# A macaron block of two expert layers and a scan layer: steps spread over other slots, the down projection turned round

## The reference, cut to what matters

```
x = x + 0.5 * ffn(layernorm(x))      # f = 0
x = x + mamba(layernorm(x))
x = x + 0.5 * ffn(layernorm(x))      # f = 1, same weights

ffn:   router = x @ Wg; top 2 of 8 experts, softmax of their logits -> w (tokens x 8)
       y  = sum_e w_e * (silu(x @ W1_e) * (x @ W2_e)) @ W3_e      (H = 176)
       y += (silu(x @ Ws1) * (x @ Ws2)) @ Ws3                      (HS = 352)
mamba: x_in, z = split(x @ W_in + b_in);  xc = silu(conv4(x_in) + conv_b)
       B, C = split(xc @ W_xp + b_xp);  delta = softplus(xc @ W_dt + b_dt)
       h_t = exp(delta_t * A) * h_{t-1} + delta_t * xc_t * B_t     (16 states)
       y_t = sum_s h_t[s] * C_t[s];  y = (y + D * xc) * silu(z)
       out = layernorm_ab(x + y @ W_out + b_out)
```

## Time and profile before

| what | us |
|---|---|
| median of three runs | 2236.86 |
| lowest and highest of them | 2232.0 and 2238.75 |
| the profiled execution | 2241.29 |
| its span, first to last instruction | 2239.5 |
| first scan of the first group starts at | 148.2 |
| twelve full iterations, k = 2 to 13 | 358.6 to 1942.5 |
| mean granted clock of TensorE, of full speed | 0.887 |

### The profile page before, as it was taken

One profiled execution on the slowest core, in us unless ns is written; L12 is line 12 of the kernel. 1 busy time (PEld: TensorE's weight loads), 2 busy tenths in 40 slices (PEclk: granted clock), 3 DMA queues, 4 the chain that ended last, 5 costly groups with the idle time before them and its releaser, 6 DMA issues.

```text
span 2239.5 us, 22836 instructions
## 1 busy us (share of the span) xinstructions
PE 1794.9 (80%) x4674; PEld 804.4 (36%) x4674; DVE 1639.6 (73%) x2505; ACT 1535.3 (69%) x2083; POOL 1441.3 (64%) x1286
## 2 busy tenths in 40 slices
PE   3878587979888888887888798788888878885577
PEld 1433233434334333333433343333333433332233
DVE  2257878687786878878687877878778786879742
ACT  1257587777778767786876778687677867776522
POOL 3346676666667675776767666676766676676753
PEclk9989788989898898998989898898989889897698
DMA  4117565555556555555555654655556555557642
GB/s 130 45 55 178 119 164 130 144 133 143 127 142 153 130 135 134 152 132 151 152 137 129 152 143 127 151 147 140 130 131 159 131 145 138 133 122 173 150 111 61
DMA packets 119129, 300.05 MB, mean 134 GB/s; under 512 B 19184, under 2 KB 40400, under 8 KB 104656
## 3 DMA queue, kind: packets, MB, share of 16 engines
q0 software_dynamic: 18432, 125.84, 28.1%
q1 hardware_dynamic: 92672, 168.88, 24.2%
q10 hardware_dynamic: 7888, 4.09, 0.7%
HBM read 167.67 MB, written 5.24 MB: 77 GB/s over the span
## 4 chain that ended last, share of the span: by engine, by line
PE 43%; ACT 21%; DVE 17%; issue 12%; POOL 3%; ACTq 1%; DMA 1%; DVEq 0%; POOLq 0%
PE ps_y L1043 9%; PE ps_h2a L1048 6%; DVE hist L868 5%; PE ps_m L1003 5%; ACT L680 5%; PE ps_h1a L1030 4%; PE ps_h1b L1030 4%; ACT L657 4%; PE ps_h2b L1048 4%; DVE den L912 3%; ACT decay L657 3%; ACT silu L680 2%; DVE yacc L950 2%; PE ps_m L1110 2%; DVE ps_db L834 2%
## 5 line engine op out<-in xcount | busy, mean ns | idle before, releaser
L569 POOL TENSOR_TENSOR prod<-hist,crow 128x1024 f32<-128x1024 f32 x224 | 556.0, 2482 | 371.8 <-DVE hist L868 368.0
L1043 PE MATMUL ps_y<-gated,down_w 128*128 128x512 f32 (+1 forms) x896 | 517.6, 664 | 101.3 <-POOL gated L521 63.2
L868 DVE TENSOR_TENSOR_SCAN hist<-decay,ps_db 128x1024 f32<-128x1024 f32 x256 | 583.2, 2278 | 13.8 <-issue 11.3
L521 POOL TENSOR_TENSOR gated<-gated,silu 128x512 f32<-128x512 f32 x352 | 476.3, 1416 | 138.1 <-DVE gated L860 108.4
L834 DVE TENSOR_TENSOR ps_db<-du,ps_db 128x1024 f32<-128x1024 f32 x256 | 313.7, 1225 | 319.1 <-PE ps_db L1012 318.8
L657 ACT ACTIVATE decay<-delta,a_neg 128x510 f32<-128x510 f32 x512 | 338.1, 711 | 2.6
L1048 PE MATMUL ps_h2a<-xnT,up_w 128*128 128x512 f32 (+1 forms) x448 | 253.2, 649 | 53.3 <-DVE gated L860 53.3
L680 ACT ACT_TABLE_LOAD x227 | 291.2, 1283 | 5.5 <-issue 0.7
L1043 PEld LDWEIGHTS ps_y<-gated,down_w 128*128 128x128 f32 (+1 forms) x896 | 180.3, 209 | 319.3 <-issue 218.0
L1030 PE MATMUL ps_h1a<-xnT,up_w 128*128 128x512 f32 (+1 forms) x448 | 248.0, 636 | 49.7 <-ACT silu L680 48.8
L657 ACT ACT_TABLE_LOAD x217 | 278.4, 1283 | 3.8
(11 more groups left out here) (137 smaller groups left out, 2242.5 us busy)
## 6 DMA issues: line engine op xcount, KB each, us to landing
yacc<-prod POOLq DMA_DIRECT2D x112, 1024.0 KB, 9.0
crow<-c_rows SPq DMA_DIRECT2D x128, 512.0 KB, 4.2
wrow<-w_rows SPq DMA_DIRECT2D x320, 128.0 KB, 3.6
wrow<-w_rows SPq DMA_DIRECT2D x64, 224.0 KB, 3.2
wrow<-w_rows SPq DMA_DIRECT2D x64, 192.0 KB, 3.6
wrow<-w_rows SPq DMA_DIRECT2D x64, 160.0 KB, 3.4
yacc<-yacc POOLq DMA_DIRECT2D x16, 512.0 KB, 6.2
wrow<-w_rows SPq DMA_DIRECT2D x64, 96.0 KB, 3.3
```

The costliest lines, as they stand in the source:

```text
L521: nc.gpsimd.tensor_tensor(gated[:, pos % NGATE, :], gated[:, pos % NGATE, :], silu[:, (pos + NCHUNK * f_parity(k, f)) % NSILU, :], ALU.mul ...
L569: nc.gpsimd.tensor_tensor(prod[:, (pair - 1 + odd) % 2, s % 2, :, :], hist[:, s % 2, :, :], c_all, ALU.mult).then_inc(prod_done, 1)
L868: nc.vector.tensor_tensor_scan(hist[:, s % 2, :, :].rearrange("p h t -> p (h t)"), decay[:, s % NA, :, :, :].rearrange("p h b t -> p (h b ...
L1043: nc.tensor.matmul(ps_y[:], down_w[0:rd, jd, :], gated[0:rd, posd % NGATE, :], start=(posd == 0), stop=(posd == NCHUNK - 1)).then_inc(down ...
```

## The change

The steps of `PLAN` stand in other slots, and some are cut in parts.

- The units start at slots 1 to 9, 11, 12 and 14 to 16 (f = 1) and 18 to 31 (f = 0). Take, join and down projection keep their lags of 1, 2 and 4 slots and run over into the next iteration.
- The down projection and the output projection are turned round: the tokens are the stationary operand, 128 at a time, and the weights move, 128 columns at a time. The result has tokens on partitions. The steps `y0`, `y1`, `yT0`, `yT1`, the copy of `outproj` and `outT` are gone; VectorE adds `ps_y` and `ps_m` directly. `addy0`, `addy1` and `resid` stand ahead of the scan of their slot. The bias `b_out` comes in as one more matmul of three bf16 rows.
- The routing weights are made on GpSimd, seven instructions at slots 16 and 29 (`weights0`, `weights1`); VectorE only finds the top two.
- `norm2` writes to two `x1n` buffers that are kept; the second normalisation for the residual (`x1n` on ScalarE) is gone, and SP copies the buffer into `rtok` by a DMA (`keep_x1n`, slot 20).
- `gate_y` is two halves at slots 7 and 8, each a multiply-add and a multiply. `delta` (slot 24) and `du` (slot 28) are apart, the convolutions and the final norm on GpSimd are cut over two and three slots, softplus's Exp stands behind the decay of slot 20 and its Ln at slot 22.
- The decays of the next group's first two states are made at slot 28; the others stay one state every second slot.

```
     PLAN = {
+        0: ["stats0"], 1: ["scale0"], 2: ["norm0"], 3: ["fold"], 4: ["addy0", "xT0"], 5: ["stats2", "scale2", "logits0"],
+        6: ["norm2", "rcopy0"], 7: ["gate_y0", "xT2"], 8: ["gate_y1"], 9: ["outproj"], 10: ["resid", "in0a"],
+        11: ["in0", "route0"], 12: ["stats3", "in1a"], 13: ["in1", "scale3"], 14: ["in2", "ln_norm"],
+        15: ["in3", "ln_scale"], 16: ["weights0"], 17: ["dt0"], 18: ["wT0", "ln_shift"], 19: ["dt1", "ln_add"],
+        20: ["sp_exp"], 21: ["addy1", "xproj", "stats1"], 22: ["scale1", "sp_ln", "bparts"], 23: ["norm1", "cT"],
+        24: ["bT", "delta"], 25: ["xT1"], 26: ["logits1"], 27: ["rcopy1", "route1"], 28: ["du"], 29: ["weights1"],
+        31: ["wT1"],
     }
...
-    UP1, UP0, BACK = 0, 14, 4
+    EARLY = ("addy0", "addy1", "resid")
+
+    UNIT = {s: (1, pos) for pos, s in enumerate((1, 2, 3, 4, 5, 6, 7, 8, 9, 11, 12, 14, 15, 16))}
+    UNIT.update({18 + pos: (0, pos) for pos in range(NCHUNK)})
+    GATE, JOIN, BACK = 1, 2, 4
...
+        13: ["w1:10"], 15: ["c5"], 19: ["store_w0", "w0:0", "w0:1", "c6", "w0:2", "w0:3"], 20: ["keep_x1n"],
+        22: ["store_x"], 23: ["w0:4", "c7"], 24: ["w0:5"], 25: ["w0:6"], 26: ["w0:7"], 27: ["w0:8"],
...
+                        elif step == "keep_x1n" and scans(k):
+                            sp.wait_ge(norm_ready[2], k + 1)
+                            if tail(k):
+                                sp.wait_ge(mamba_added, k)
+                            sp.dma_start(rtok[:], x1n[odd][:]).then_inc(x1n_ready, 16)
...
+                            chain.link(nc.gpsimd.tensor_tensor(drop[:], top[:, :, 1], top[:, :, 0], ALU.subtract))
+                            chain.link(nc.gpsimd.tensor_tensor(edrop[:], euler[:], drop[:], ALU.pow))
+                            chain.link(nc.gpsimd.tensor_tensor(den[:], edrop[:], pow_mone[:], ALU.subtract))
+                            chain.link(nc.gpsimd.tensor_tensor(prob[:, :, 0], den[:], pow_mone[:], ALU.pow))
+                            chain.link(nc.gpsimd.tensor_tensor(prob[:, :, 1], edrop[:], prob[:, :, 0], ALU.mult))
...
-                    if slot == SLOTS - 1 and lead(k):
+                    if slot == SLOTS - 4 and lead(k):
                         decays(k + 1, nxt, range(NA // 2))
...
-                        nc.tensor.matmul(ps_y[:], down_w[0:rd, jd, :], gated[0:rd, posd % NGATE, :], start=(posd == 0),
-                                         stop=(posd == NCHUNK - 1)).then_inc(down_done, 1)
+                        for t in range(TILES):
+                            ins = nc.tensor.matmul(ps_y[:, t * C:(t + 1) * C],
+                                                   gated[0:rd, posd % NGATE, t * P:(t + 1) * P], down_w[0:rd, jd, :],
+                                                   start=(posd == 0 and t == 0),
+                                                   stop=(posd == NCHUNK - 1 and t == TILES - 1))
+                        ins.then_inc(down_done, 1)
...
+                            xr = xres[:, oldest if f else ahead, :, :].rearrange("p t c -> p (t c)")
+                            nc.vector.scalar_tensor_tensor(xr, ps_y[:], 0.5, xr, ALU.mult, ALU.add
+                                                           ).then_inc(y_taken, 1)
```

305 lines of the change are left out of this document (154 added, 151 removed), and 12 rows, old and new, of tables (PLAN, SP_PLAN).

## The result

| | before | changed |
|---|---|---|
| median, us (4 runs each, side by side) | 2234.43 | 2182.60 |
| lowest and highest | 2231.74 and 2238.75 | 2179.17 and 2186.16 |
| ratio of the runs, with its 95% interval | | 0.9766, 0.9739 to 0.9793 |
| span of the profiled execution | 2239.5 | 2177.1 |

The account below looks back on a forecast made before the run. Each pair was taken as bound by whichever engine has most there. Between 110.0 and 121.9 per iteration it took 116.8, plus 1.2: 118.0, 14.0 less; 14 x 14.0 = 196 off 2236.9 gives 2041 us, 8-in-10 range 1945 to 2200.

Parts of the forecast that it names:

- the levelling: Work spread more evenly over each iteration's sixteen pairs; pairs 3, 9, 11 and 14 at 7 to 10 us.
- VectorE's and GpSimd's work: Busy time per iteration: VectorE summed at 110.6 before, 101.8 changed; GpSimd +4.0 us.
- The down projection with the tokens stationary: TensorE, each unit: eight 128-column passes at 0.11, 0.90 us against 0.86 before, loads hidden.
- that rival: Down projection's weight loads not hidden: 0.219 us per pass, 1.75 per unit, kernel slower at 2273; chance 0.04.
- The sum: Dearest engine per pair, summed over an iteration: 110.0 with two engines, 121.9 with four; changed kernel placed between, at 116.8.
- The holds: VectorE's two-SBUF-input steps lengthened by GpSimd: 5.9 us in sum, 0.84 each, plus 1.2 for closer packing.
- The rival that sums holds: Seven VectorE steps held longer by GpSimd; gain gone past 2.1 us mean, 2283 at 2.5; chance 0.06.
- GpSimd's weights: Routing weights on GpSimd: pairs 8 and 14 at 8.3, delay covered; otherwise 1 to 3 us in pairs 9 and 15.
- Moves at nothing: Moved steps priced at zero: addy and resid ahead of the scan, and the keep_x1n copy on SP.
- The ramps: Part-filled iterations at the kernel's start and end: four at half the gain, counted as two more.
- The less-gain one: Rival: every pair costs its dearest engine, 121.9 per iteration, 2096 us; chance 0.25, tail to 2200.
- no change: Rival: stalls come back elsewhere (late wrow, turns of ps_m), 2237 us; chance 0.03.

Follow-up runs that it names:

- gate_psum_weights_one: Changed kernel with gate_y's second inputs read from PSUM and six of seven GpSimd weight instructions per route left out (output wrong); 2033.34 us.
- The best kernel here: Changed kernel with both gate_y steps ahead of a scan and GpSimd's routing weights at even slots 12 and 28; 2108.93 us.
- gate_psum: Changed kernel with the second input of all four gate_y instructions read from PSUM instead of SBUF (output wrong); 2104.36 us.
- gate_before_scan: Changed kernel with the two gate_y steps ahead of the scans of slots 6 and 8 instead of behind one; 2142.03 us.
- gate_early: Changed kernel with the two gate_y steps one slot earlier, at slots 6 and 7; 2174.91 us.

## Why the prediction was right or wrong

- **Direction and the levelling: right.** Pairs 3, 9, 11 and 14 were to be 7 to 10; they are 7.9, 11.4, 8.5 and 5.6. Pair 9 is over it, and 3.0 of it are the weights; pair 14 is under it.
- **VectorE's and GpSimd's work: right in its change**, -8.9 and +4.2 per iteration. VectorE's level was 7 too high on both sides (110.6 and 101.8 summed, 103.4 and 94.5 measured).
- **The down projection with the tokens stationary: right.** Eight passes were to take 0.90. TensorE in pair 4:

```profile
762.44 1.05 PE L1058 MATMUL ps_y<-down_w,gated 128*128 128x128 f32 x8
763.33 1.02 PE L1066 MATMUL ps_h2a<-xnT,up_w 128*128 128x512 f32 x2
```

  0.89 from start to start, 0.11 per pass; the weight loads are hidden, and that rival is out. The granted clock rose from 0.90 to 0.94.
- **The sum: the step that failed.** Before, the time lay 0.57 of the way between the maxima of two engines and of four, and I put the changed kernel at the same place between 110.0 and 121.9. It came to 126.9, outside of both. A maximum over engines supposes that their work in a pair overlaps. In pair 4 it doesn't: gate, projection, row of B and product of B are on three lists, each behind the one before, and the pair costs their sum: 12.7 where the dearest engine was to have 7.4. In that row lie two things that the sum had at nothing, the hold as something that TensorE waits for, and the projection at a granted clock of 0.51 behind that wait, 1.6 us. The position of before said nothing on that, since the change brings the ends of this chain together: `gate_y` as a whole at slot 6 and `outproj` at 8 before, the last half at slot 8 and `outproj` at 9 now.
- **The holds: their sum right, their place wrong.** The sum had the two-input steps of VectorE at their durations of before and 1.2 us more for closer packing. Per full iteration `gate_y` went from 4.8 to 6.5 and the first cast from 1.7 to 2.3, but `du` from 3.3 to 1.2 and `delta` from 1.7 to 1.2: together 11.2 after 11.4, so even the 1.2 was too much. What cost was not more holding but holding on `gate_y`: its steps are held 3.6 per iteration and cost 5.2, because TensorE waits for them, while `du` lost about 2 us of hold. The rival that sums holds (it decides from 2.1 us each) was not met either: `gate_y`'s four instructions are held 0.9 each. A hold is to be priced by who waits for the step, not by the busy time of its engine.
- **GpSimd's weights: the cover was looked for at the wrong place.** I had the delay in pairs 8 and 14, as GpSimd's own load (8.3 each), covered by the double `hist`, with 1 to 3 us in pairs 9 and 15 if it is used up. Pairs 8 and 14 are 5.6. The delay comes out in pairs 9 (3.0), 15 (1.7) and 0 (2.1): through the joins in pair 9 and in part in pair 0, through `wT1` in pair 15, for neither of which TensorE's list has such a cover. What was a doubt in that step was the rule.
- **"Moves at nothing": true of `addy`, nearly so of `resid`.** VectorE idles 6.9 us before `addy` and 1.7 us before `resid` in the whole changed run. But TensorE waits 1.1 us per iteration in pair 5 until `resid` has taken `ps_m` (none before), which is most of that pair's 1.4 over its figure; with `resid` later that wait is gone and pair 6 is longer by as much. And the sentence left out what stands ahead of `resid`, and with that the chain of pair 4. The places of `gate_y`, `outproj` and `wT1` had no term at all.
- **The ramps: too much.** I counted the part-filled iterations as two more. The first one takes 97.2 where it took 96.7, and twelve iterations make 61.1 of the 62.4 us. In gate_psum_weights_one, 181.4 of 204.8 us are from the twelve. There, they are worth 1.5.
- **The rivals.** The less-gain one (2096, every pair at its dearest engine) is 87 us short. The nearest in time is "no change" (2237, 54 us off), given 0.03, and its reason, stalls that come back elsewhere, is nearest to what happened: 14.0 of 19.1 us came back, though not at the places that it names (late `wrow`, turns of `ps_m`). That the time lies in the range for 8 in 10 is owed to the tail of the less-gain rival, not to a mechanism that was foreseen. That gate_psum_weights_one, 2033, lies beside the forecast of 2041 does not confirm the pairs one by one: pair 1 was to be 7.1 and is 9.8, pair 11 was to be 10.1 and is 8.5.

**Open.** The best kernel here still has pairs of 9.4 (3), 10.4 (1) and 10.5 (15). The last varies from 6.2 to 15.9 between iterations; TensorE's weight loads wait 3.4 us per iteration for joins there, where it was 1.4 in the changed kernel, and `weights1` now stands at slot 28, but what makes it vary no run here explains. Nor was it tried to make `gate_y` read an operand from PSUM with the right values.

## What to carry to other kernels

A step whose result another engine needs in the same stretch is to be priced as a chain (this step, held; what waits for it; what stands behind that on its list), and the sum of maxima only for the rest. Where a VectorE step with two SBUF inputs must run beside GpSimd, put it where nobody queues behind it; a PSUM operand took the hold away here, in a kernel that for that computed other values. When small steps go to a third engine, ask whose inputs come later on that engine's list: here three other pairs paid for them, and in a slot ahead of a long wait one of the two cost nothing.

## What the runs showed of the hardware

- **A hold lasts over more than one instruction of GpSimd.** Above, L901 took 3.60 while two joins ran (2.82 together) and ended 0.56 behind the second; the earlier trace rows show the same over a product and a join. The Trainium skill (SBUF — State Buffer, "SBUF: two separate sides") speaks of one whole instruction of the other engine; here it was the row of them.
- **A PSUM operand frees a VectorE step from it**: 2.8 us for four steps against 6.5, among the same GpSimd work.
- **TensorE after a wait**: the same sixteen passes took 3.50 in the mean at a granted clock of 0.51, behind an idle time of 3.83, in the changed kernel, and 1.89 at 1.00, behind 0.15 and 0.0, in gate_psum and gate_before_scan, in each of twelve iterations. The wait cost itself and then the slower matmuls behind it. In gate_early the idle time (2.79) stands one matmul group earlier, and the passes take 3.0 at 0.64.
- **The seam of the loop.** The iterations 2 to 13 are six turns of a loop whose body holds two; those before and behind are written out. In the changed kernel pair 15 takes 7.5 in the middle of a turn and 10.2 to 10.3 at its end, in the five turns that another follows. TensorE, ScalarE and VectorE at that seam:

```profile
857.35 2.07 PE L1058 MATMUL ps_y<-down_w,gated 128*128 128x128 f32 x8 [3.32 <-issue]
857.44 1.28 ACT L669 ACT_TABLE_LOAD   x1 [2.92 <-issue]
858.00 0.69 DVE L877 TENSOR_TENSOR gated<-ps_h2b,wrow 128x512 f32<-128x512 f32 x1 [2.70 <-issue]
```

  All three stand still for 2.7 to 3.3 us and wait for nothing that the profile shows. Before has it too (its pair 15 takes 4.1 and 6.0 to 6.9 in turn), so it doesn't explain the difference; it is some 2.7 us a turn in the changed kernel, 14 us of the whole. At the end of the sixth turn, where the same instructions run and no jump back follows, pair 15 takes 7.5 and none of the three engines has such a stall; nor has it in the written-out iterations 1 and 14 (7.5 and 7.4). So the stall goes with the jump back and not with every second iteration. What in the jump takes the time no run here shows.
